# A decoder's scan stage: input products into PSUM by VectorE, output products of both lanes by GpSimd, B and C rows broadcast by DMA

## The reference, cut to what matters

```
u, res = x @ W_in split in two halves of 256 channels;  u = silu(u)
delta  = softplus(u @ W_delta + b_delta)
Bm, Cm = u @ W_B, u @ W_C                    # 16 states each
A      = -exp(A_log)                         # 256 x 16
h[t]   = exp(delta[t] * A) * h[t-1] + delta[t] * B[t] * u[t]     # 256 x 16 per token
y[t]   = sum over the 16 states of h[t] * C[t]
y      = (y + u * D_param) * silu(res);  out = y @ W_out
```

## Time and profile before

| | us |
|---|---|
| three runs | 1264.33, 1267.41, 1274.64 |
| median | 1267.41 |
| span of the profiled execution, first to last instruction | 1266.5 |
| VectorE busy in it | 988.6 (78%) |
| TensorE busy in it | 885.7 (70%) |
| ScalarE busy in it | 570.6 (45%) |
| GpSimd busy in it | 256.6 (20%) |

### The profile page before, as it was taken

The page is one execution under the profiler, slowest core; times in us unless marked ns, Lnnn a source line. Parts: engine busy times, 40 slices in busy tenths (PEclk is TensorE's granted clock), DMA queues, the critical chain, the costliest instruction groups (busy, mean ns, idle before and its releaser), DMA issues. The chain is left out here.

```text
span 1266.5 us, 10862 instructions
## 1 busy us (share of the span) xinstructions
PE 885.7 (70%) x3174; PEld 451.5 (36%) x3176; DVE 988.6 (78%) x1819; ACT 570.6 (45%) x1593; POOL 256.6 (20%) x125
## 2 busy tenths in 40 slices
PE   2551557767889868988826227676789996798893
PEld 1440312223346424444314112222243653344342
DVE  1278789998469579999816876999964975999993
ACT  1413353331434356865812146333333443966782
POOL 5011015554242010000000210555521501000000
PEclk9665578888989879999967568788899887999997
DMA  7100000000000000000010000000000000000000
GB/s 211 30 0 1 0 1 0 0 1 0 1 1 1 1 1 1 1 1 1 1 48 1 1 0 1 0 0 1 1 1 1 1 1 0 1 1 1 1 0 17
DMA packets 17403, 10.31 MB, mean 8 GB/s; under 512 B 6084, under 2 KB 16058, under 8 KB 17338
## 3 DMA queue, kind: packets, MB, share of 16 engines
q1 hardware_dynamic: 15368, 7.59, 2.2%
q10 hardware_dynamic: 1970, 1.97, 0.6%
HBM read 8.50 MB, written 1.05 MB: 8 GB/s over the span
## 5 line engine op out<-in xcount | busy, mean ns | idle before, releaser
L883 ACT ACTIVATE mem<-ps 77x512 f32<-77x512 f32 (+3 forms) x192 | 115.5, 603 | 387.4 <-POOL mem L1479 148.9
L1463 POOL TENSOR_TENSOR rs<-ve,minus_half 128x4 f32<-128x4 f32 (+2 forms) x60 | 102.0, 1709 | 811.5 <-DVE ve L1081 683.2
L851 PE MATMUL ps<-mem,ident 128*128 128x512 f32 x512 | 231.4, 600 | 30.5 <-DVE mem L1431 29.7
L1041 ACT ACTIVATE mem<-mem 128x32 f32<-128x32 f32 x1024 | 217.8, 308 | 0.0
L703 PE MATMUL ps<-mem,ident 128*128 128x512 f32 x256 | 154.9, 737 | 79.8 <-POOL mem L1479 79.8
L1479 POOL TENSOR_TENSOR mem<-mem 128x1024 f32<-128x1024 f32 x32 | 136.0, 4250 | 181.5 <-DVE mem L1267 181.5
L1431 DVE SCALAR_TENSOR_TENSOR mem<-mem 128x1024 f32<-128x1024 f32 x128 | 159.1, 1278 | 13.4 <-ACT mem L1041 12.0
L851 PEld LDWEIGHTS ps<-mem,ident 128*128 128x128 f32 x512 | 93.9, 190 | 167.1 <-issue 92.7
L1267 DVE TENSOR_TENSOR_SCAN mem<-mem 128x1024 f32<-128x1024 f32 x64 | 142.9, 2274 | 0.0
L1423 DVE TENSOR_TENSOR mem<-mem 128x1024 f32<-128x1024 f32 x96 | 112.9, 1216 | 0.3
L703 PEld LDWEIGHTS ps<-mem,ident 128*128 128x128 f32 x256 | 56.7, 233 | 157.1 <-POOL mem L1479 97.0
(11 more groups left out here) (223 smaller groups left out, 1269.9 us busy)
## 6 DMA issues: line engine op xcount, KB each, us to landing
x<-in_x_dram SPq DMA_DIRECT2D x4, 256.0 KB, 3.7
out_dram<-x SPq DMA_DIRECT2D x4, 256.0 KB, 2.3
mask<-in_mask_BxSxS_ik_dram SPq DMA_DIRECT2D x4, 154.0 KB, 3.5
mem<-n_L_ffn_expert_down_dram SPq DMA_DIRECT2D x1, 512.0 KB
mem<-in_L_xattn_Wo_dram SPq DMA_DIRECT2D x1, 512.0 KB
mem<-in_L_xattn_Wv_dram ACTq DMA_DIRECT2D x1, 512.0 KB
a_q<-in_L_xattn_Wq_dram SPq DMA_DIRECT2D x1, 512.0 KB, 4.4
a_k<-in_L_xattn_Wk_dram SPq DMA_DIRECT2D x1, 512.0 KB, 4.9
```

The costliest lines, as they stand in the source:

```text
L851: mm = pe.matmul(ps[:, j, :], ident[:], WH[s][:, h % WB, j * 512:(j + 1) * 512], start=(h == 0), stop=(h == PH - 1), skip_group_check=True)
L883: ins = nc.scalar.activation(to, of, ACT.Copy, **kw)
L1041: ins = nc.scalar.activation(SVA[s][:, n % 2, i * NK:(i + 1) * NK], sims[:, 1, h, :], ACT.Identity, bias=sims[:, 0, h, i:i + 1])
L1463: nc.gpsimd.tensor_tensor(RS[s][0:rows, i * n:(i + 1) * n], VE[s][0:rows, i * n:(i + 1) * n], minus_half[0:rows, 0:n], ALU.pow)\
```

## The change

- In the scan stage VectorE writes the input products of both lanes into PSUM (banks 2 and 3 of the lane) and its scan reads them from there. The y sum moves to banks 0 and 1.
- GpSimd makes the output product of both lanes; VectorE makes none.
- B and C no longer go through bf16 parts and matmuls. ScalarE copies the 32 rows to SBUF (BCR), SyncE writes them to DRAM (bc_rows), and for each n SyncE broadcasts one row of B and one of C to all partitions by DMA into double buffers (BQ and CQ). VectorE and GpSimd read them from SBUF.
- row_pick and the instructions that make it go, and so does ScalarE's copy of C.
- BLEND_LANES is empty. The code behind `if s in BLEND_LANES` is not built into the program.

```diff
+    BLEND_LANES = ()
+    bc_rows = [nc.dram_tensor(f"bc_rows{s}", (2 * NS, S), F32, kind="Internal").ap() for s in range(LANES)]
-        row_pick = sb("row_pick", [96, 2 * NS, P], BF16)
@@ GpSimd, before the loop
-                w.link(nc.gpsimd.memset(row_pick[:], 0.0))
-                for g in range(3):
-                    w.link(nc.gpsimd.affine_select(
-                        out=row_pick[:], in_=row_pick[:], compare_op=ALU.not_equal, fill=1.0,
-                        base=-2 * NS * g, pattern=[[-1, 2 * NS], [0, P]], channel_multiplier=1))
@@ SyncE, in the loop
+                    def broadcasts(s):
+                        w = Signals(sp)
+                        yield 0
+                        w.next(sg["bc_sb"][s])
+                        sp.dma_start(bc_rows[s], BCR[s][:]).then_inc(sg["bc_out"][s], 16)
+                        yield 0.5
+                        w.next(sg["bc_out"][s], 16)
+                        for n in range(NS):
+                            yield 1 + n
+                            slot = n % 2
+                            if s not in BLEND_LANES:
+                                if n >= 2:
+                                    w.next(sg["dbu_done"][s])
+                                sp.dma_start(BQ[s][:, slot, :], down(bc_rows[s][n, :]))\
+                                    .then_inc(sg[("B_even", "B_odd")[slot]][s], 16)
+                            if n >= 2:
+                                w.next(sg["hc_done"][s])
+                            sp.dma_start(CQ[s][:, slot, :], down(bc_rows[s][NS + n, :]))\
+                                .then_inc(sg[("C_even", "C_odd")[slot]][s], 16)
+
+                    in_turn(broadcasts)
@@ TensorE, scan
-                    w.next(G("bcs_ready", s))
-                    w.next(G("delta_ready", s))
-                    broadcast(0, 0, "B_ready")
-                    broadcast(NS, 3, "C_ready")
                     for n in range(NS):
...
                         w.next(G("hc_done", s))
...
                         for j in range(DJ):
-                            mm = pe.matmul(ps[:, 1 + j, :], ident[:], HC[s][:, n % 2, j, :],
+                            mm = pe.matmul(ps[:, j, :], ident[:], HC[s][:, n % 2, j, :],
                                            start=(n == 0), stop=(n == NS - 1), skip_group_check=True)
@@ ScalarE, scan, behind the two Abs of stage 2
+                    w.next(G("bc_ready", s))
+                    copy(BCR[s][:], ps[0:2 * NS, 3, :], G("bc_sb", s))
...
-                        if s == POOL_LANE:
-                            yield 3.6 + n
-                            w.next(G("C_ready", s))
-                            if n >= 1:
-                                w.next(G("hc_done", s))
-                            copy(CSB[s][:], ps[:, 3, :], G("c_sb", s))
@@ VectorE, scan
-                    (the five bf16 splits of lines 1236 to 1240)
+                    dbu = ps[:, 2:4, :]
+                    if s not in BLEND_LANES:
+                        w.next(G("delta_ready", s))
+                        w.next(G("bc_sb", s))
                     for n in range(NS):
-                        yield 4 + n
-                        w.next(G("B_ready", s))
-                        nc.vector.tensor_tensor(dBu[s][:], DU[s][:], spread(ps[:, 0, :], 1, DJ), ALU.mult)\
-                            .then_inc(G("dbu_done", s), 1)
+                        if s not in BLEND_LANES:
+                            yield 4 + n
+                            w.next(G(("B_even", "B_odd")[n % 2], s), 16)
+                            if n >= 1:
+                                w.next(G("scan_done", s))
+                            nc.vector.tensor_tensor(dbu, DU[s][:], spread(BQ[s][:, n % 2, :], 1, DJ), ALU.mult)\
+                                .then_inc(G("dbu_done", s), 1)
                         yield 4.2 + n
                         w.next(G("dbu_done", s))
                         w.next(G("dA_ready", s))
-                        hs = (HS, TU)[n % 2][s]
-                        if s == POOL_LANE and n >= 2:
+                        if n >= 2:
                             w.next(G("hc_done", s))
-                        nc.vector.tensor_tensor_scan(hs[:].rearrange(flat), dA[s][:, n % 2].rearrange(flat),
-                                                     dBu[s][:].rearrange(flat), 0.0, ALU.mult, ALU.add)\
-                            .then_inc(G("scan_done", s), 1)
-                        if s == POOL_LANE:
-                            continue
-                        yield 4.4 + n
-                        w.next(G("scan_done", s))
-                        w.next(G("C_ready", s))
-                        if n >= 2:
-                            w.next(G("y_acc", s))
-                        nc.vector.tensor_tensor(HC[s][:, n % 2], hs[:], spread(ps[:, 3, :], 1, DJ), ALU.mult)\
-                            .then_inc(G("hc_done", s), 1)
+                        nc.vector.tensor_tensor_scan((HS, TU)[n % 2][s][:].rearrange(flat),
+                                                     dA[s][:, n % 2].rearrange(flat), dbu.rearrange(flat), 0.0,
+                                                     ALU.mult, ALU.add).then_inc(G("scan_done", s), 1)
@@ GpSimd, scan
-                    if s == POOL_LANE:
-                        for n in range(NS):
...
+                    for n in range(NS):
+                        yield 304.45 + n
+                        w.next(sg["scan_done"][s])
+                        w.next(sg[("C_even", "C_odd")[n % 2]][s], 16)
+                        if n >= 2:
+                            w.next(sg["y_acc"][s])
+                        nc.gpsimd.tensor_tensor(HC[s][:, n % 2], (HS, TU)[n % 2][s][:],
+                                                spread(CQ[s][:, n % 2, :], 1, DJ), ALU.mult)\
+                            .then_inc(sg["hc_done"][s], 1)
```

More of the change, by code:

```diff
@@ L87, in decoder @@
     GB = 3
-    POOL_LANE = 0
+    BLEND_LANES = ()
+    XT_TURNS = 6
     ACT_HEADS = (4, 7)
@@ L180, in decoder @@
         ST = lanes(sb, "st", [P, 6, NB])
-        WORDS = 12600
+        WORDS = 14000
         mem = lanes(sb, "mem", [P, WORDS])
@@ L219, in decoder @@
             qt=(P, (S,), BF16), hq=(P, (NB, F), BF16), ht=(P, (NB, FK, P), BF16))
-        TU, TR, UU, SPA, SPE, DL, DU, BCS, BC1, BCM, dBu, HS, HC = per_lane(
+        TU, TR, UU, SPA, SPE, DL, HS, HC, CQ, BQ, BCR, BT, DU = per_lane(
             tu=(P, (DJ, S), F32), tr=(P, (DJ, S), F32), uu=(P, (DJ, S), F32), spa=(P, (DJ, S), F32),
[L223 to L227, removed]
+            spe=(P, (DJ, S), F32), dl=(P, (DJ, S), F32), hs=(P, (DJ, S), F32), hc=(P, (2, DJ, S), F32),
+            cq=(P, (2, S), F32), bq=(P, (2, S), F32), bcr=(2 * NS, (S,), F32), bt=(P, (NB, NS), F32),
+            du=(P, (DJ, S), F32))
         _, dA = per_lane(front=(P, (3 * DJ * S,), F32), da=(P, (2, DJ, S), F32))
+        _, DUT, _, DZ = per_lane(front=(P, (9 * DJ * S + 2 * S,), F32), duT=(P, (NB, DI), F32),
+                                 rows=(P, (S + NB * NS,), F32), dz=(P, (2, NB, DI), F32))
         AT, SC, MX, RD = per_lane(
@@ L678, in scan @@
                     mm.then_inc(G("bc_ready", s), 1)
[L680 to L685, removed]
-                    w.next(G("bcs_ready", s))
-                    w.next(G("delta_ready", s))
-                    broadcast(0, 0, "B_ready")
-                    broadcast(NS, 3, "C_ready")
-                    for n in range(NS):
[L691 to L694, removed]
+                    if s in BLEND_LANES:
+                        for k in range(NB):
+                            for j in range(DJ):
+                                mm = pe.matmul(ps[:, 0, k * NS:(k + 1) * NS], UU[s][:, j, k * P:(k + 1) * P],
+                                               m_bc[:, j, 0:NS], start=(j == 0), stop=(j == DJ - 1))
+                        mm.then_inc(G("bc_ready", s), 1)
+                        yield 2.8
+                        w.next(G("delta_ready", s), 2)
+                        w.next(G("bc_sb", s))
+                        for k in range(NB):
+                            for j in range(DJ):
+                                at = k % 2 * DI + j * P
+                                mm = pe.transpose(ps[:, 2 + k // 2, at:at + P], DU[s][:, j, k * P:(k + 1) * P], ident[:])
+                        mm.then_inc(G("turned", s), 1)
@@ new lines, in scan @@
+                    for n in range(NS):
+                        if s in BLEND_LANES:
+                            yield 3.7 + n
+                            w.next(G("dz_ready", s))
+                            if n == 0:
+                                w.next(G("xT_ready", s))
+                            else:
+                                w.next(G("scan_done", s))
+                            for j in range(DJ):
+                                for k in range(NB):
+                                    mm = pe.transpose(ps[:, 2 + j, k * P:(k + 1) * P],
```

(26 more changed lines are left out.)

28 lines of the change are left out of this document (9 added, 19 removed).

## The result

The changed kernel takes 1296.48 us in the median of 4 runs (1289.81 to 1299.65), the kernel before, with a fourth run added, 1265.87 (1261.69 to 1274.64). The forecast was 1293. The profiled execution has a span of 1298.0 us and a device time of 1299.65, so it is the longest of the four; the span is 31.5 us above the one before.

A forecast was written before the change was run, and what follows sets the result against it. VectorE's queue was taken to set the step's length. Steps +30.3, stage start +3.4, stage end -4.0 and prologue -3.0 sum to +26.7 on 1266.5, so 1293 us; own range 1278 to 1302, with rivals 1246 to 1304.

The forecast's parts named there:

- The product's own time: GpSimd's output product in a step: 2.29 us by itself, the rest of its 4.25 us being waiting.
- rival 3: GpSimd's output product really takes 4.25 us, so GpSimd's queue sets the period at 8.55 and the time at 1288; chance 0.05.
- The steady step: Scan stage: period 8.95 us against 7.94, +1.01 a step, +30.3 us over thirty periods.
- the two prices of VectorE's wait: VectorE's wait for a whole GpSimd product: 1.7 us scaled from a short row, or 2.15 us; 2.15 was taken.
- the upper end: VectorE waits 2.15 us for a GpSimd product, its 2.29 less 0.14.
- The hand-over: Scan steps: GpSimd's second product gets in between VectorE's two back-to-back input products; the forecast's case, chance 0.60.
- first rival: Scan steps: VectorE keeps the port, GpSimd slips behind both input products; period 7.0, time 1235 us; chance 0.15.
- Stage start: Start of each scan stage: ScalarE's copy of the B and C rows ahead of Exp costs +1.7 us a pass, +3.4.
- Prologue: Before the loop: GpSimd's memset and selects go, the last load releases the first matmul near 18.0, -3.0 us.
- Stage end: End of each scan stage: lane 1's last combine starts 7.0 instead of 9.0 us after scan 0, -4.0 in all, bounds -4 to +2.
- Broadcasts and SyncE: DMA broadcasts of B and C rows: hidden, the first by 2 to 3 us; SyncE has no other work there.

The follow-up runs named there:

- half product: The changed kernel with GpSimd's lane 1 product covering 512 of 1024 columns, TensorE adding that half twice: 1264.03 us in one run.
- deferred kernel: The changed kernel with one added wait: GpSimd's lane 1 product waits for VectorE's lane 1 input product of the next step; 1234.85 us, ratio 0.9775 to before.
- copy on VectorE: The deferred kernel with the B and C rows copied to SBUF by VectorE instead of ScalarE: 1229.69 us, ratio 0.9710 to the kernel before.
- matmuls doubled: The changed kernel with each matmul adding an output product to y done twice, except in the last step: 1292.4 us in one run.

## Why the prediction was right

*The product's own time.* 2.29 us was worked out from the stretch of the power instructions; it is 2.35 beside a scan with one SBUF input. The trace of before had booked 4.25 for it, and a reader of that row alone would have had GpSimd as the bound (rival 3).

*The steady step.* Predicted 8.95, measured 8.99, with every piece in its place: input products of 1.42 and 3.37 us, products of 2.35 and 3.33. Over both passes the steps cost 31.8 us more (15.6 and 16.1), the term was +30.3. The choice between the two prices of VectorE's wait was the right one: the second input product is 2.15 us longer, the upper end, and the half product shows that the wait goes by columns.

*The hand-over.* The step on which forecast and first rival parted was that GpSimd gets in between two back-to-back multiplies of VectorE. One row of the trace of before spoke for it. Resting on one row, it got 0.60 and not more. The changed kernel's rows show that it does, 3.33 and then 3.37 us, and the deferred kernel that without it the time is 1235. The rows need no rule of a hand-over for it: product 1 has started 1.05 us before the second input product (184.64 against 185.69) and is served before it. In all collisions shown here the instruction that had started first had the port first, by 0.05 us in the kernel before with both products on GpSimd.

*Stage start.* +1.7 us a pass predicted, +1.73 measured in both passes; the copy on VectorE takes that back (6.41 to 4.67).

*Prologue.* -3.0 predicted, -3.2 measured, released by the load that was named.

*Stage end: mis-sized.* -4.0 predicted for both passes, -1.3 measured (-0.8 and -0.5). The products and the order were right; the last eight matmuls took 5.40 us in both passes and not 3.70, at a granted clock between the two levels, 0.69 in pass 1. That lay inside the bounds given (-4 to +2), but the value taken was the end of the range and had assumed the level of the earlier trace rows for a TensorE with less to do. Why the clock was lower there is only partly shown. With the matmuls doubled it is full speed in both passes. But it is full speed too at the stage ends of the deferred kernel and of the one with lane 1's product on VectorE, which have no broadcast matmuls either, and the latter has the same 0.80 in its steps; the half product kernel has full speed in one pass and not in the other.

*Broadcasts and SyncE.* Hidden, as said; the margin for the first one was 5.6 us (168.33 + 3.8 against 177.70), not 2 to 3, since the store to DRAM and the broadcast both landed sooner than the rows they were taken from.

The terms measured add to 31.8 + 3.5 - 1.3 - 3.2 = 30.8 of the 31.5 us between the spans; of the other 0.7 us, 0.5 lie behind the second scan stage.

## What to carry to other kernels

A duration in the profile can hold a wait. Before work is handed to an engine because its share is low, look for what its instruction takes beside different neighbours; the shortest with the same shape is the price, the rest is a collision. When instructions of two engines exclude each other, it is the order in which they start that decides, and a wait that costs nothing in itself (the deferred product) can be worth more than the multiply that it lets GpSimd take over (2.0 us a step against 1.2). And when an edit changes how much TensorE has to do, the time of matmuls that something waits for needs bounds at both levels of its clock.

## What the runs showed of the hardware that was not expected

- VectorE's wait for GpSimd is 2.1 ns a column in products of 512 and 1024 columns (1.07 and 2.15 us), and 1.6 in a power instruction of 16 columns (26 ns).
- VectorE pays nothing for writing a product to PSUM, or for scanning from it: 1226 ns at the least for the input product (1226 into SBUF), 4.45 us for the pair of scans against 4.47.
- A wait is the rest of the other engine's instruction less 0.11 to 0.16 us, on either side. VectorE loses 0.07 us of duration where the product has 0.21 us to go (lane 1's product on VectorE), and 0.20 of 0.33 and 2.15 of 2.28 in the changed kernel; GpSimd loses 0.98 of 1.13 there.
- A GpSimd power instruction of 16 columns does not hold VectorE for its 2.90 or 3.46 us: the two-SBUF multiply that starts while it runs is 26 ns longer than the median.
- Of TensorE's clock, 0.80 was granted in the steps of pass 1 of the changed kernel and 0.83 in those of the kernel before; with the matmuls doubled, 0.94 in the window shown. Without the broadcast matmuls and with the shorter step of the deferred kernel it was 0.89 in 182:270.
